# q^T and k^T kept in SBUF as f32, 16 rows of each head in 32-partition groups, in a fused attention and mixture-of-experts layer

## What is computed

```python
qp = q @ Wq.T
kv = latent_kv @ Wkv_expand.T
k, v = jnp.split(kv, 2, axis=-1)
qh = qp.reshape(b, sq, NH, HD).transpose(0, 2, 1, 3)
kh = k.reshape(b, sk, NH, HD).transpose(0, 2, 1, 3)
scores = jnp.einsum('bhqd,bhkd->bhqk', qh, kh) * inv_sqrt_d
scores = jnp.where(causal, scores, jnp.finfo(scores.dtype).min)
attn = jax.nn.softmax(scores, axis=-1)
out = jnp.einsum('bhqk,bhkd->bhqd', attn, vh)
```

## Time and profile before

| What | Value |
|---|---|
| Median of 3 runs | 255.47 us (255.03 to 255.53) |
| Span of the profiled execution | 253.9 us |
| Mean granted TensorE clock | 0.879 |
| PE busy | 190.2 us (75%) |
| DVE busy | 126.7 us (50%) |
| POOL, ACT busy | 88.4 us, 76.0 us |
| DMA share of the chain that ended last | 23%, and 11% in SyncE's queue |

### The profile page before, as it was taken

The page is one execution under the profiler, slowest core; times in us unless marked ns, Lnnn a source line. Parts: engine busy times, 40 slices in busy tenths (PEclk is TensorE's granted clock), DMA queues, the critical chain, the costliest instruction groups (busy, mean ns, idle before and its releaser), DMA issues.

```text
span 253.9 us, 3767 instructions
## 1 busy us (share of the span) xinstructions
PE 190.2 (75%) x1319; PEld 135.6 (53%) x1319; DVE 126.7 (50%) x354; ACT 76.0 (30%) x165; POOL 88.4 (35%) x119
## 2 busy tenths in 40 slices
PE   8589068749983989604899878989899999988000
PEld 3455045426561658403569556868597887766000
DVE  3857027727551794402964727468746665423000
ACT  2133001326630472201651654142203332222000
POOL 7304700124325330000520431000605888867710
PEclk9689759968997699965999979999999999999655
DMA  6419999985799519991011010399511555554556
GB/s 174 135 51 150 118 193 119 158 260 171 186 145 228 221 48 283 146 134 27 3 41 46 3 41 0 105 307 293 177 56 44 83 82 82 79 82 51 62 60 126
DMA packets 32286, 30.28 MB, mean 119 GB/s; under 512 B 2508, under 2 KB 27372, under 8 KB 32268
## 3 DMA queue, kind: packets, MB, share of 16 engines
q1 hardware_dynamic: 28320, 23.26, 45.8%
q0 software_dynamic: 3744, 6.69, 14.2%
q10 hardware_dynamic: 204, 0.10, 0.2%
HBM read 21.15 MB, written 9.83 MB: 122 GB/s over the span
## 4 chain that ended last, share of the span: by engine, by line
PE 32%; DMA 23%; DVE 13%; SPq 11%; issue 8%; POOL 8%; ACT 1%; POOLq 0%; DVEq 0%; ACTq 0%
DMA q_rows<-q_parts_d 10%; DMA out<-y_rows,tok_i 6%; SPq L374 5%; PE m_ps L1332 4%; PE s_ps L1188 4%; PE s_ps L1191 4%; SPq L367 4%; DVE top L803 3%; PE s_ps L1316 3%; DMA q_rows<-shift_t 3%; POOL out L542 2%; PE t_ps L1218 2%; POOL k_parts L530 2%; PE o_ps L1236 2%; POOL odd_d L542 2%
## 5 line engine op out<-in xcount | busy, mean ns | idle before, releaser
L803 DVE TENSOR_REDUCE top<-s_ps 128x2 f32<-128x512 f32 (+1 forms) x48 | 32.2, 687 | 37.6 <-PE s_ps L1191 37.3
L481 POOL TENSOR_SCALAR_AFFINE_SELECT probs<-probs 128x256 f32<-128x256 f32 (+1 forms) x48 | 23.3, 486 | 64.5 <-ACT probs L594 62.8
L594 ACT ACTIVATE probs<-t_ps 128x512 f32<-128x512 f32 x48 | 27.7, 596 | 32.6 <-PE t_ps L1218 29.4
L1188 PE MATMUL s_ps<-mask_b,ident_b 128*128 128x256 bf16 (+1 forms) x48 | 18.6, 388 | 22.3 <-DMA q_rows<-q_parts_d 19.9
L1316 PE MATMUL s_ps<-xn_t,sgu 128*128 128x256 f32 (+1 forms) x96 | 23.5, 385 | 0.0
L1191 PE MATMUL s_ps<-k_rows,q_rows 96*128 96x128 bf16 (+1 forms) x128 | 21.5, 283 | 0.0
L1218 PE MATMUL t_ps<-q_rows,k_rows 99*128 99x256 bf16 x64 | 13.8, 310 | 9.4 <-DMA q_rows<-shift_t 9.1
L1188 PEld LDWEIGHTS s_ps<-mask_b,ident_b 128*128 128x128 bf16 x48 | 5.3, 110 | 27.5 <-issue 21.5
L1316 PEld LDWEIGHTS s_ps<-xn_t,sgu 128*128 128x128 f32 (+1 forms) x96 | 16.5, 182 | 3.4 <-issue 0.6
L1191 PEld LDWEIGHTS s_ps<-k_rows,q_rows 96*128 96x128 bf16 x128 | 13.9, 119 | 5.4 <-issue 4.2
L470 POOL TENSOR_TENSOR k_parts<-rest,k_parts 128x512 bf16<-128x512 f32 x3 | 3.5, 1154 | 36.6 <-DVE k_parts L787 19.4
(11 more groups left out here) (166 smaller groups left out, 382.7 us busy)
## 6 DMA issues: line engine op xcount, KB each, us to landing
k_rows<-k_parts_d SPq DMA_DIRECT2D x24, 128.0 KB, 6.4
q_rows<-q_parts_d SPq DMA_DIRECT2D x24, 128.0 KB, 8.2
wgu_early<-in_w_gu SPq DMA_DIRECT2D x8, 352.0 KB
k_parts_d<-k_parts SPq DMA_DIRECT2D x4, 384.0 KB, 7.1
q_parts_d<-q_parts SPq DMA_DIRECT2D x4, 384.0 KB, 6.9
wdn_early<-in_w_dn SPq DMA_DIRECT2D x8, 176.0 KB
q_rows<-in_w_gu SPq DMA_DIRECT2D x4, 352.0 KB
v_ones<-in_w_gu SPq DMA_DIRECT2D x4, 352.0 KB
```

The source lines that it names most:

```text
L481: nc.gpsimd.affine_select(out=v, in_=v, compare_op=ALU.is_ge, fill=0.0, base=0, pattern=[[0, v.shape[1]], [1, P]], channel_multiplier=-1). ...
L594: t_ring.emptied(nc.scalar.activation(probs[:, g % 2, u, :], t_ring.bank(job)[:], ACT.Exp, scale=HD ** -0.5), job)
L803: s_ring.emptied(nc.vector.tensor_reduce(dst, src, AX.X, ALU.max), job)
L1188: nc.tensor.matmul(masked, ident_b[:], mask_b[:].unsqueeze(1).to_broadcast([P, len(heads), P]), start=True, stop=False, skip_group_check=True)
```

## The change

The round trip is gone. `wk_wide` and `wq_wide` hold the projection weights spread out with zeros, so that each projection gives, for four heads at a time, k^T or q^T with 16 rows of each head in a 32-partition group (`RG`). The result is copied as f32 to `k_t` and `q_t`. Row 16 of each group is one in `k_t` and, after `add_shift`, minus the maximum in `q_t`. The maxima are written into `top` at a stride of 32 and turned by `turn_shift`, two f32 jobs of four matmuls each. A score product is now one f32 matmul of 16 rows, a transposed one of 17. Projections of k and q need two jobs each, with twice the matmuls. Units are emitted in pairs (`side_by_side`): both masks and waits first, then the products in turn, the two units in different 32-row groups; `S_BESIDE` and `S_FIRST` choose the partners. The projections of batches 2 and 3 move one batch later. The idle products go from 39 to 14. The weights of experts 0 to 7 are issued at the start; experts 8 to 11 and gathered rows get tiles of their own.

```diff
-KEEP_BUSY = {("k", 0): 11, ("q", 0): 3, ("x", 1): 2, ("q", 1): 4, ("s", 0, 0): 10, ("shift", 0): 9}
+KEEP_BUSY = {("k", 0, 0): 11, ("x", 0): 3}
...
+S_BESIDE = ((1, 2, 3), (0, 8, 10), (4, 6, 11), (5, 7, 9))
+
+S_FIRST = ((0, 1), (2, 3), (4, 6), (8, 10), (5, 7), (9, 11))
+FIRST_FILL = ((), (("x", 1),), (("k", 1, 0), ("k", 1, 1)), (("q", 1, 0), ("q", 1, 1)), (("v", 0),), (("v", 1),))
...
-            constant(nc.gpsimd.memset(k_rows[SPLIT_ROWS:P].rearrange("r b h t -> r (b h t)").bitcast(F32),
-                                      1.0 + 0x3F80 / 2 ** 23))
...
+                m_ring.emptied(nc.scalar.activation(
+                    q_t[:, b % 2, 2 * i:2 * i + 2, :].rearrange("p j t -> p (j t)"), m_ring.bank(job)[:], ACT.Copy), job)
...
+            def add_shift(b):
+
+                for i in range(2):
+                    job = ("shift", b, i)
+                    m_ring.wait(dve, job)
+                    rows = q_t[:, b % 2, 2 * i:2 * i + 2, :].rearrange("p j t -> p (j t)")
+                    m_ring.emptied(nc.vector.tensor_tensor(rows, m_ring.bank(job)[:], rows, ALU.add), job)
...
+                rows = slice(RG * g, RG * g + HD)
+                ins = nc.tensor.matmul(s_ring.bank(job)[:, keys * n:keys * n + keys],
+                                       q_t[rows, b % 2, j, P * qt:P * qt + P], k_t[rows, b % 2, j, 0:keys],
+                                       start=False, stop=(n == parts - 1), skip_group_check=True)
...
+            def side_by_side(first, second):
+                for job in (first, second):
+                    if job[0] == "st":
+                        begin_scores_t(*job[1:])
+                for job in (first, second):
+                    if job[0] == "s":
+                        begin_scores(*job[1:])
+                for quarter in range(4):
+                    products(first, quarter)
+                    products(second, quarter)
...
+            before = None
+            for job, after in zip(PE_ORDER, PE_ORDER[1:] + [("end",)]):
+                if before is not None:
+                    side_by_side(before, job)
+                    before = None
+                elif after[0] == "s" and job[0] in ("s", "st"):
+                    before = job
+                else:
+                    step[job[0]](*job[1:])
```

More of the change, by code:

```diff
@@ L217, in build @@
         unread = sb("unread", [P, 1])
[L218 to L221, removed]
+        q_t = sb("q_t", [P, 2, GH, S])
+        k_t = sb("k_t", [P, 2, GH, S])
         v_ones = sb("v_ones", [P, B, QT, NH, 2 * HD])
[L223 to L226, removed]
+        top = sb("top", [P, QT, GH, NG, RG])
         probs = sb("probs", [P, 2, 3, 2 * S])
@@ L307, in build @@
         xn_ready = sem("xn_ready")
[L308 to L315, removed]
+        wide_ready = sem("wide_ready")
+        top_zeroed = sem("top_zeroed")
+        max_ready = sem("max_ready")
         probs_masked = sem("probs_masked")
@@ L349, in _ @@
                              x[b].rearrange("(t p) c -> p t c", p=P)).then_inc(x_in[b], 16)
[L351 to L373, removed]
-                        sp.dma_start(q_rows[row:row + HD, b % 2], src[part]).then_inc(rows_in["q"][b % 2], 16)
-                        row += HD
             def store_base(b):
@@ L697, in fill @@
                         filling[job[0]](*job[1:])
+            for jobs in FIRST_FILL:
+                fill(jobs)
             for b in range(B):
@@ L1157, in turn_x, with queries @@
                 m_ring.filled(last, job)
[L1159 to L1160 removed]
+            def queries(b, i):
+                job = ("q", b, i)
                 m_ring.begin(pe, job)
[L1162 to L1165 removed]
+                if i == 0:
+                    m_ring.wait_emptied(pe, ("x", b))
+                if b == 0 and i == 0:
+                    pe.wait_ge(wide_ready, 6)
+                for n in range(2):
@@ new lines, in turn_shift, with begin_scores_t @@
+                for n in range(2):
+                    for qt in range(QT):
+                        o = S * n + P * qt
+                        last = nc.tensor.matmul(m_ring.bank(job)[:, o:o + P],
+                                                top[:, qt, 2 * i + n].rearrange("p g r -> p (g r)"), minus_ident[:],
+                                                start=True, stop=True)
+                m_ring.filled(last, job)
+            def begin_scores_t(b, g, u):
+                if g == 0 and u == 0:
+                    for i in range(2):
+                        m_ring.wait_emptied(pe, ("shift", b, i))
+                t_ring.begin(pe, ("st", b, g, u))
@@ L1227, in outputs, with alone @@
+            def alone(*job):
+                begin_scores_t(*job)
+                for quarter in range(4):
+                    products(("st", *job), quarter)
             def outputs(b, g):
```

326 lines of the change are left out of this document (132 added, 194 removed), and 4 rows, old and new, of the table TAIL_FILL.

## The result

| | before | after |
|---|---|---|
| Median of 5 runs each, us | 255.53 (255.03 to 259.00) | 323.33 (321.52 to 329.50) |
| Span of the profiled execution, us | 253.9 | 327.8 |
| Mean granted TensorE clock | 0.879 | 0.739 |
| PE busy, us | 190.2 | 294.9 |

The change makes the kernel slower by a factor of 1.266 (95% interval 1.2595 to 1.2727).

A forecast was written before the change was run, and what follows sets the result against it. DMA was taken to bound the starts, PE the units. First transposed unit at 42 us, then stages, tails and batch 3 to 206.7, plus 100.8, gave 307.5; with 1.6 added, 309 us. Range 250 to 330, the forecast case's own 291 to 328.

The forecast's parts named there:

- Start: Kernel start up to the first scores: they begin at about 15.5 us instead of 34.17, queries taken at 5 us.
- Batch 0 alone: First scores to first transposed unit: 21.6 us at full clock plus 5 for half clock, ending at 42 us.
- Cost of a unit: Each score or transposed unit: 0.87 us at 2.4 GHz, 1.7 at 1.2; two in different row groups overlap fully.
- Stages: Three stages of twelve paired units and three output products: 17 us full clock, 32 half; 28, 28.5 and 28.5 taken.
- Which clock: Paired stages: TensorE falls to half clock after some 5 us, because units use about a quarter of the array.
- The rival that goes by it: Whole kernel: busy TensorE keeps full clock, stages of about 17 us, total 252 us; chance 0.13.
- Tails: Work after each paired stage: 17, 22.5 and 15.2 us, the first two including 3 us for a half-clock first part.
- Batch 3: Batch 3's lone transposed units: about 24 us and 1 behind, half clock after some 3 us, instead of 11.57.
- Rest: Routing and experts at the end: 100.8 us, taken over unchanged.
- the full clock throughout: Rival for the whole kernel: clock stays full while TensorE is busy, total 252 us; chance 0.13.
- full clock in pairs and half in batch 3's units: Rival: paired stages at full clock, batch 3's lone units at half, total 262 us; chance 0.17.
- The groups that do not overlap: Rival: a pair's row groups run one after another; 289 us at full clock, 364 at half; chance 0.14.

The follow-up runs named there:

- e11: e10 with 31 idle products in place of 17, ahead of all six pairs of batch 0's first scores and the values of batch 1: median 250.73 us.
- e3: The changed kernel with partners chosen so that both units of a pair lie in the same 32-row group: 386.12 us (1 run).
- e1: The changed kernel with score and transposed products on all 32 rows of their group, added rows zero on one side: median 275.24 us, 1.068 of before.
- e2: The changed kernel, still 16 and 17 rows, with two idle 128-row products ahead of each transposed unit: median 304.60 us, 1.195 of before.
- e5: e1 plus two idle products ahead of each of batch 3's 12 lone transposed units: 270.13 and 274.60 us.
- e8: e6 with the second unit of each batch 3 pair in a score-ring bank and more idle products before the first stage: median 261.19 us, 1.019 of before.
- e6: e1 with batch 3's transposed units paired, one idle product per pair, batch 0's values earlier, four idle products before batch 1's transposes: median 284.46 us.
- e10: e8 without masks in the score units, plus three idle products ahead of five of batch 0's six first-score pairs: median 255.09 us, 0.981 of before.
- e4: The changed kernel with all products of a pair's first unit issued before the second's, instead of in turn: 333.84 us (1 run).

## Why the prediction was right, and where it was mis-sized

The forecast was 309 (own range 291 to 328), the measured median 323.33: slower, for the reason given, and 14 us more than forecast. Against the span the sum was 307.5, and the profiled execution has 327.8. By the steps of the prediction:

- **Start.** First scores at 15.5; the trace has the first mask at 14.66. The queries were taken between the clocks at 5 us and took 3.69, at full clock. Right within an us, and in part by luck: the transposes came at 8.86 for 8.5, but not because of x. Without the memset VectorE's operation on x is done by 6.82. The transposes stood behind the keys (6.14 to 8.20) and behind three idle products on PE, which the sum had not counted; the rows are from the timeline of after.

```profile
6.09 0.73 DVE L705 TENSOR_SCALAR xn<-xs,mv,rstd 128x256 f32<-128x256 f32 x2
...
8.20 0.82 PE L1031 MATMUL m_ps<-ones_b 128*128 128x512 bf16 x3
...
8.86 0.60 PE L1073 MATMUL m_ps<-ident,xn 128*128 128x128 f32 x4
```

- **Batch 0 alone.** Forecast 26.5, measured 45.40 - 14.66 = 30.74, PEclk 0.67. Here the term was mis-sized: 5 us had been put on a stretch at half clock, and the clock was half from 16.7 to 33.8 and again from 40.6 to 44.0; the stretch took 9.1 more than the 21.6 of full clock. The working at full clock, 21.6, stands near e11: 25.30 less 35 idle products of 0.22 us is 17.7, and 19.5 with the masks that e11 leaves out; the idle products also cover waits, so the true figure is above that. The first transposed unit came at 45.4, not 42: 3.4 us.
- **Cost of a unit.** Full overlap of two row groups was assumed: shown, by common starts and by e3 (4.25 at half clock with a long mask, 2.55 with two groups). The section "Key Properties" of "TensorEngine Tiling (Array Packing)" in the Trainium skill states that tiles work independently; the trace agrees, with starts 10 ns apart. The pair was put at 1.29 with a long mask at full clock and took 1.40; at half clock 2.25 and 2.46 were expected, 2.34 and 2.55 measured. Two changes of 0.1 had been counted, and a third was paid, as above.
- **Stages.** 28, 28.5 and 28.5 forecast, 31.54, 30.80 and 30.50 measured: 7.8 us in all. About 1 us of each is the 0.1 for each pair. Most of the rest is the clock: 5 us at full clock had been allowed, and it fell 2.0 us into the first stage, 4.0 and 4.4 into the others.
- **Which clock.** That it falls though PE is never idle was right: PE is busy for 31.54 of 31.54 us at 0.53, and e1 shows that the rows used are the reason. The ground given for it was thinner than it reads: in both stretches of the earlier trace rows PE was also idle for 1.5 of 3.40 us, and half of the records of the first one were not 64-row matmuls but idle products on 128 rows, so these rows could not tell idle time from unused array. Only e1 and e2 do. The rule of the Trainium skill cited there ("TensorE: Matmul & The Clock Gate", section "Why this matters for your kernels": keep TensorE busy without gaps) does not hold here, and the measurement decides: PE had no gap in these 31.54 us. The rival that goes by it came to 252.
- **Tails.** 17, 22.5 and 15.2 forecast, 17.65, 23.42 and 15.08 measured. The 3 us put on a first part at half clock was about right.
- **Batch 3.** 24 and 1 behind it forecast; its units took 25.88 (in the earlier trace rows 11.57 before). The clock fell at 197.6, 3.2 us in, with 3 assumed. Right.
- **Rest.** 100.8 forecast, 107.53 measured, a miss of 6.7. Of it 2.2 us are the last output product and the shared expert's product beside it, up to the first transposes of the output: 4.94 us at 0.53, where before had 2.76 at full clock. The other 4.5 lie behind 225.21: 102.59 us to the end, where before has 98.06, at a mean clock of 0.90 and 0.91. I had taken this part over unchanged, and the change need not be what lengthens it: from the same transposes of batch 3's output to the end, with the same 477 matmul records, e1 took 98.88 us (176.22 to 275.10), e5 97.27 (171.13 to 268.40) and e11 103.48 (147.92 to 251.40). So 4.5 us lie within what this part varies by between executions; the profiled one of after is the longest of its five.

The differences are 3.4 for the way to the first transposed unit, 7.8 for the stages, 1.5 for the tails, 0.9 for batch 3 and 6.7 for the rest: 20.3, which is 327.8 - 307.5. The profiled execution is 6.2 over the median; the median itself is 14 over the forecast.

Of the rivals, the full clock throughout is what e11 needed 32 rows, another bank plan, no masks and idle products to get, up to 175.5 us; full clock in pairs and half in batch 3's units is not what after does, but it is just what e1 does (275.24, where 262 had been worked out with the pairs at 1.18). The groups that do not overlap are e3, at 386.12 for the 364 worked out.

## What to carry to other kernels

Before replacing split bf16 products by f32 ones on small row groups, ask two things of the trace: how many more columns PE streams, and how much of the array is at work while it does. A PE that is 100% busy on an eighth or a quarter of the rows can be held at half clock; here filling each head's group to 32 rows with zeros cost nothing and gave 48 us back. Look also at what stands ahead of such a stage, since its own work may hold a full clock that it cannot bring back: with four idle products there the profiled first stages of e8 to e11 stayed full. That is a hint and not a proof, as e1's did so without them.

## What was unexpected in the hardware

- Zeros count: 32 rows, of which 15 or 16 contribute nothing, kept PEclk at 1.00 for a stage of 18.28 us where 16 and 17 rows gave 0.53, with the same instructions.
- The same work can have either clock. The same 32-row pairs held 1.00 for a whole stage (e1), and stayed at 0.50 for the rest of one once it had fallen 2.2 us in (e6).
- Added work can shorten a stage: with 24 idle products it took 23.46 instead of 31.54 us (e2). In the first scores the profiled execution with more of them took 25.30 instead of 30.47 (e11 and e10), though there the clock also differs between executions of one kernel.
- Row groups run side by side even when one unit's products are all issued before the other's (2.34 us for a pair, e4), if both have the same shape.
